# Strip copies on SyncE's queue: from the end of one turn to behind the next turn's map loads

## The chip, the cores and the metric

The kernel runs on one core of one Trainium2 chip. The metric is the device time of one execution in microseconds (us), lower is better. Everything is float32. The engines are PE (matrix), DVE (vector), ACT (scalar), POOL (GpSimd) and SP (SyncE, which only issues DMAs here). PEld is PE's weight load. DMAs are issued from SP, ACT and POOL. The profile shows three queues for them: q1 carries what SP issues, q10 what ACT issues, q0 what POOL issues. All three share the core's 16 DMA engines.

## The reference

The input x is 16 samples of 128 channels of 160 x 160 pixels. Per sample:

```python
x_proj = einsum('bchw,oc->bohw', x, proj_w)          # 128 -> 64 channels
att1 = _route(x_proj, ..., [3x3, 5x5], dilation 1)   # depthwise, one of two kernels
att2 = _route(att1, ..., [7x7, 9x9, 11x11], dilation 3)
out = concatenate([att1, att2], axis=1)
att = concatenate([out.mean(1), out.max(1)])         # two maps
att = sigmoid(conv7x7(att, sp_w) + sp_b)
gate = att[:, 0:1] + att[:, 1:2]
return out * gate + x
```

`_route` takes the mean of its input over all pixels, multiplies it with a small matrix, and uses the depthwise kernel of the largest logit. So the first convolution of a sample can't begin before the whole sample has been read and summed.

## The kernel before

The samples are pipelined in 18 turns, s = 0 to 17. In turn s, PE does in this order: the projection of sample s (`project`, L958, and the transposes `turn_x`, L967, in 30 pieces, five for each of six bands of rows), the routing of sample s (`route`, L1002 and L1009), the first convolution of sample s (`conv1`, L1022 and L1023, 32 pairs of channels) and then the second convolution of sample s-1 (`conv2`, L1086). Between the pairs of the first convolution stand the finishing steps of older samples: `finish2` (L1054 on PE, L1395 on DVE) gates the second half of the output of sample m = s-2 and adds x, `finish1` (L1065, L1420) does this for the first half of sample n = s-3. Turns 3 to 15 do all of this for new samples, thirteen turns. Turn 2 has no `finish1`. Turn 16 has no new sample but still a second convolution, turn 17 has neither.

The gate of sample m is made at the beginning of turn s. PE turns the two maps of sample m (`turn_map2`, L979), DVE writes them to Mt (`spread2`, L1337), SP stores Mt to map2_d in DRAM with twelve small DMAs (`store_map2`, L439), before these it reads the maps of the first half (L430), and behind them it reads the maps back in another layout (`load_maps`, L445). DVE joins both (`combine`, L1343 to L1346). PE convolves (`spatial`, L1032), ACT takes the sigmoid (L855), DVE adds (`sum_gate`, L1350). SP stores the gate (L465) and loads it with six DMAs in a third layout (L473). DVE copies it (`spread_gate`, L1358), PE turns it (`turn_gate`, L1040) and DVE takes it (`take_gate`, L1368). PE executes `turn_gate` behind the fourth pair of the first convolution, so a late gate stops the first convolution there. On DVE, `combine` stands ahead of the last band's sum (`take_x`, L1206 to L1211), and this stands ahead of the routing.

The bands 3 to 5 of x are loaded by POOL (L643) at the beginning of the turn: bands 3 and 4 at once, band 5 after band 3 has been used. ACT loads the first convolution's weights for five pairs ahead as soon as the routing is done (`load_w1`, L827), and in the second convolution it loads the weights of each pair (`load_w2`, L861).

Between the two convolutions a sample goes through DRAM. SP stores the first convolution's result to nat_d (`store_att1`, L488). `make_strips` (L538) then copies nat_d to strip_d, DRAM to DRAM, as 18 DMAs of 6.4 MB together. `land` (L478) loads strip_d into L for the second convolution. `land(s-1, u)` needs L freed by `finish2` and so comes in pieces late in the next turn. Before, `make_strips(s)` is SP's last step in turn s: behind `early_pieces` (L495, L502, L508), which run with the end of the second convolution. The next turn's `store_map2` follows on the same queue.

`wait_alone(engine, semaphore, value)` lets an engine wait. SP executes its list in order, so what stands behind a wait is issued after it.

Of the kernel before, what the change touches and what calls it, by code (L numbers as in the profile page):

```python
# [80 lines left out]
def conv_block(nc, x, proj_w, w1, b1, w2, b2, att1_w, att1_b, att2_w, att2_b, sp_w, sp_b, out):  # L81
    B = x.shape[0]
    ctx = ExitStack()
    with ctx:
# [188 lines left out]
        def wait_alone(eng, s, value):  # L273

            if isinstance(value, int) and value <= 0:
                return
            eng.wait_ge(s, value)
            eng.sem_inc(waits_met)
# [87 lines left out]
        def row_groups(r):  # L366

            return ((0, 48), (48, 6 if r == 0 else 5))
# [4 lines left out]
        def _(sp):  # L373
# [47 lines left out]
            def store_map2(m):  # L421

                for mm in range(2):
                    wait_alone(sp, map2_evac, 6 * m + 3 * mm + 3)
                    if mm == 0:
                        if isinstance(m, int) and m == 0:
                            sp.wait_ge(s_zeroed, 16 * NZ)
                        wait_alone(sp, map1_stored, 64 * (m + 1))
                        for k in range(2):
                            sp.dma_start(m1[64 * k:64 * k + 48, :, :],  # L430
                                         bass.AP(map1_d.tensor, m * (2 * 168 * W) + k * 168 * W, [[W, 48], [SPB * W, 4], [1, W]])
                                         ).then_inc(min_loaded, 16)
                    for cg in range(2):
                        for k in range(3):
                            n = 10 if (cg, k) == (1, 2) else 30
                            dst = bass.AP(map2_d.tensor, m * (2 * 168 * W) + (mm * 168 + 3) * W + 90 * cg + 30 * k,
                                          [[18 * W, BR], [W, 18], [1, n]])
                            src = Mt[k:NT:3, mm, 540 * cg:540 * cg + 540].rearrange("p (r j) -> p r j", j=30)[:, :, 0:n]
                            sp.dma_start(dst, src).then_inc(map2_stored, 16)  # L439

            def load_maps(m):
                wait_alone(sp, map2_stored, MP2 * (m + 1))
                wait_alone(sp, sp_mm, 2 * m)
                for k in range(2):
                    sp.dma_start(minc[64 * k:64 * k + 48, :, 3:3 + W],  # L445
                                 bass.AP(map2_d.tensor, m * (2 * 168 * W) + k * 168 * W, [[W, 48], [SPB * W, 4], [1, W]])
                                 ).then_inc(min_loaded, 16)

            def load_xf(m, u):
                for par in range(2 if u < 4 else 1):  # L450
                    n = min(ROWS2, H - 36 * u - 18 * par)
                    sp.dma_start(xf[u % 2][64 * par:64 * par + 64, 0:n * W],
                                 x[m, C2:C, 36 * u + 18 * par:36 * u + 18 * par + n, :].rearrange("c h w -> c (h w)")
                                 ).then_inc(xf_loaded[u % 2], 16)

            def store_xf(m, u):
                sp.wait_ge(f2_add, 45 * m + 9 * (u + 1))
                for par in range(2 if u < 4 else 1):
                    n = min(ROWS2, H - 36 * u - 18 * par)
                    sp.dma_start(out[m, C2:C, 36 * u + 18 * par:36 * u + 18 * par + n, :].rearrange("c h w -> c (h w)"),  # L460
                                 xf[u % 2][64 * par:64 * par + 64, 0:n * W]).then_inc(out2_stored[u % 2], 16)

            def load_gate(m):
                wait_alone(sp, gate_sum, m + 1)
                sp.dma_start(gate_d[m, 0:H, :].rearrange("(b i) w -> i b w", i=SPB),  # L465
                             sg[:, 0, :].rearrange("p (b w) -> p b w", w=W)).then_inc(gate_stored, 16)
                wait_alone(sp, gate_stored, 16 * (m + 1))
                for cg in range(2):
                    for k in range(3):
                        n = 10 if (cg, k) == (1, 2) else 30  # L470
                        src = bass.AP(gate_d.tensor, m * (168 * W) + 90 * cg + 30 * k, [[18 * W, BR], [W, 18], [1, n]])
                        dst = Gt[k:NT:3, 540 * cg:540 * cg + 540].rearrange("p (r j) -> p r j", j=30)[:, :, 0:n]
                        sp.dma_start(dst, src).then_inc(g2_loaded, 16)  # L473

            def land(s, bc):
                for p, po, r, lo, hi in ((0, 0, 0, 0, 192), (1, 0, 0, 192, 320), (1, 128, 1, 0, 64), (2, 0, 1, 64, 256)):
                    src = bass.AP(strip_d.tensor, (p * BK + bc) * 54 * 1920 + po, [[192, PB], [6 * 1920, BR], [1, hi - lo]])
                    sp.dma_start(Lc[64 * r:64 * r + PB].rearrange("p (n f) c -> p n (f c)", f=5)[:, BR * bc:BR * bc + BR, lo:hi],  # L478
                                 src).then_inc(landed, 16)
# [47 lines left out]
            def make_strips(s):  # L527
                wait_alone(sp, landed, LND * s)
                if isinstance(s, int) and s == 0:
                    sp.wait_ge(s_zeroed, 16 * NZ)  # L530
                for p in range(3):
                    for p0, n in row_groups(p):
                        d0 = p * BK * 54 * 1920 + p0 * 1920
                        f0 = s * (PIX * C2) + (p + 3 * p0) * W * C2
                        for do, fo, strips, run in ((54 * 1920, 15 * C2, 4, 1920), (15 * C2, 0, 1, 960), (5 * 54 * 1920, 135 * C2, 1, 1600)):
                            mid = [[54 * 1920, strips]] if strips > 1 else []
                            mid2 = [[1920, strips]] if strips > 1 else []
                            sp.dma_start(bass.AP(strip_d.tensor, d0 + do, [[1920, n]] + mid + [[1, run]]),  # L538
                                         bass.AP(nat_d.tensor, f0 + fo, [[3 * W * C2, n]] + mid2 + [[1, run]])).then_inc(strip_stored, 16)

            def load_g1(m):
                wait_alone(sp, pr_ready, 16 * m)
                sp.dma_start(G1[:, :, :, :].rearrange("p u r j -> p (u r) j"),
                             bass.AP(gate_d.tensor, m * (168 * W), [[10, PX1], [800, 32], [1, 10]])).then_inc(g1_loaded, 16)

            def turn(t):
                s, m = t.s, t.m
                if t.two:
                    store_map2(m)
                    load_maps(m)  # L550
                    if t.new:

                        wait_alone(sp, x_summed, NB1 * s + NB1 - 1)
                        wait_alone(sp, proj_mm, NF * (NB1 * s + NB1 - 1))
                    load_xf(m, 0)
                    load_gate(m)
                    wait_alone(sp, g2_mm, m + 1)
                    load_xf(m, 1)
                    if not t.new and not t.conv2:
                        load_g1(m)  # L560
                    if t.conv2:
                        wait_alone(sp, strip_stored, SST * s)
                    for u in range(NU2):
                        store_xf(m, u)
                        if t.conv2:
                            land(s - 1, u)
                        if u < 3:
                            wait_alone(sp, out2_stored[u % 2], xf_count(m, u))
                            load_xf(m, u + 2)
                    if t.conv2:  # L570
                        land(s - 1, 5)
                elif t.conv2:

                    sp.wait_ge(s_ones, 1)
                    wait_alone(sp, strip_stored, SST * s)
                    for bc in range(BK):
                        land(s - 1, bc)
                if t.new:
                    store_att1(s)
                if t.two and (t.new or t.conv2):  # L580
                    load_g1(m)
                if t.new:
                    wait_alone(sp, att1_stored, ST1 * (s + 1))
                    wait_alone(sp, red1_steps, s + 1)
                    if t.early:
                        begin_early(m)
                    if t.next:
                        load_x2(s + 1)
                    if t.early:
                        early_pieces(m)  # L590
                    make_strips(s)

            samples(sp, turn)
            for q in range(2):
# [937 lines left out]
```

## Time and profile before

| | us |
|---|---|
| median of three runs | 6009.83 |
| lowest and highest | 5991.84, 6009.97 |
| the profiled execution | 6016.42 |
| its span | 6014.7 |
| PE busy | 4768.7 (79%) |
| DVE busy | 3136.8 (52%) |
| ACT busy | 2827.8 (47%) |
| POOL busy | 1039.5 (17%) |

Times in the trace count from the start of the span. The beginning of a turn is best read from DVE's last `spread2` instruction (L1337): its end is called S here. At S the maps of sample m stand in Mt and can be stored. S is 3385.5 in turn 10, 600.1 in turn 2 and 5484.8 in turn 16. "S + 73.8" is a time 73.8 us after that.

### The profile page before, as it was taken

How to read it: one execution, taken by the hardware profiler on the slowest of the kernel's cores; microseconds unless marked ns; L12 is line 12 of the kernel's file. 1: busy time of each engine (PE TensorE's matmuls, PEld its weight loads, DVE VectorE, ACT ScalarE, POOL GpSimd, SP SyncE). 2: the span in 40 equal slices, each digit the busy share in tenths (PEclk: the TensorE clock that was granted, in tenths of full speed). 3: DMA queues.
4: the chain of work that ended last, by engine and by line, in shares of the span. 5: the costliest groups of instructions: out<-in, count | busy, mean ns of one | idle time of the engine just before them, and what ended most of it. 6: DMA issues, size and time to landing. Idle time of an engine off the chain costs nothing.

```text
span 6014.7 us, 156600 instructions
## 1 busy us (share of the span) xinstructions
PE 4768.7 (79%) x62816; PEld 3244.4 (54%) x62816; DVE 3136.8 (52%) x3931; ACT 2827.8 (47%) x5378; POOL 1039.5 (17%) x1574
## 2 busy tenths in 40 slices
PE   5678887888878888887888888788888878885453
PEld 2336474655647465564746547474654747464453
DVE  3315455554645546474554547455464755545345
ACT  3455554544545454454545454454545445451120
POOL 2001011111112111121211111121111212111232
PEclk8889999988989989898999989899998989897675
DMA  9655787979888797988879788897978888796957
GB/s 241 185 159 172 173 209 226 230 219 224 237 210 218 216 233 218 222 244 209 218 219 235 216 222 244 200 227 213 237 219 222 246 202 224 211 213 176 221 135 198
DMA packets 1033176, 1284.58 MB, mean 214 GB/s; under 512 B 670749, under 2 KB 865736, under 8 KB 1001885
## 3 DMA queue, kind: packets, MB, share of 16 engines
q1 hardware_dynamic: 899468, 723.43, 50.5%
q0 software_dynamic: 64304, 410.01, 21.8%
q10 hardware_dynamic: 69026, 146.11, 9.5%
q8 instruction: 235, 3.85, 0.3%
q14 instruction: 143, 1.17, 0.1%
HBM read 950.16 MB, written 456.70 MB: 234 GB/s over the span
## 4 chain that ended last, share of the span: by engine, by line
PE 50%; DMA 21%; SPq 9%; DVE 8%; issue 7%; ACT 3%; ACTq 1%; POOL 1%; another core or an unknown queue 0%; DVEq 0%; POOLq 0%
PE psC L1086 19%; PE psA L1022 10%; PE psA L1023 9%; DMA RX<-w_d 6%; SPq L439 6%; DMA RX<-in_x_dram 5%; PE psB L1054 3%; PE psA L958 3%; PE psB L1065 2%; PE psB L1032 2%; DMA out_dram<-RX 2%; DMA RX<-nat_d 2%; DVE L L1375 2%; PE psB L967 2%; DMA map_d<-RX 2%
## 5 line engine op out<-in xcount | busy, mean ns | idle before, releaser
L1086 PE MATMUL psC<-RX 61*60 61x96 f32 (+7 forms) x49152 | 1479.9, 268 | 276.1 <-POOL RX L680 129.4
L1086 PEld LDWEIGHTS psC<-RX 61*60 61x60 f32 x49152 | 1412.8, 134 | 341.9 <-issue 329.2
L875 ACT ACTIVATE L<-psC 124x120 f32 (+4 forms) x2048 | 396.8, 287 | 885.6 <-PE psC L1086 830.5
L1022 PE MATMUL psA<-X,RX 128*128 128x240 f32 x1280 | 638.0, 588 | 129.7 <-ACT RX L840 128.2
L680 POOL COPY RX<-RX 64x720 f32<-64x720 f32 x512 | 426.2, 839 | 1408.8 <-DMA RX<-w_d 1407.5
L845 ACT ACTIVATE X<-psA,bias 128x246 f32<-128x246 f32 x1024 | 626.6, 722 | 56.2 <-issue 25.6
L1054 PE MATMUL psB<-ident,L 124*128 124x124 f32 x2160 | 381.1, 318 | 334.9 <-DVE RX L1395 163.7
L1310 DVE TENSOR_REDUCE MM<-L 124x135 f32<-124x2160 f32 (+1 forms) x192 | 535.3, 2844 | 212.7 <-ACT L L875 212.7
L1395 DVE TENSOR_TENSOR RX<-psB,RX 128x360 f32<-128x360 f32 (+7 forms) x1200 | 359.2, 350 | 546.5 <-PE psB L1054 485.6
L1023 PE MATMUL psA<-X,RX 128*128 128x240 f32 x1280 | 632.5, 583 | 0.0
L865 ACT ACTIVATE RX<-L 128x1080 f32 (+1 forms) x256 | 542.4, 2127 | 147.8 <-DMA L<-strip_d 147.7
L958 PE MATMUL psA<-RX,projt 128*64 128x512 f32 x1600 | 460.4, 657 | 158.1 <-DMA RX<-in_x_dram 102.7
L834 ACT ACTIVATE RX<-RX 32x640 f32<-32x640 f32 x320 | 234.5, 737 | 744.6 <-PE psA L1023 665.3
L1054 PEld LDWEIGHTS psB<-ident,L 124*128 124x128 f32 x2160 | 295.7, 167 | 470.4 <-issue 460.3
L1286 DVE TENSOR_REDUCE MM<-X 128x246 f32<-128x15744 f32 x16 | 264.8, 16553 | 465.6 <-ACT X L845 465.6
L798 ACT ACTIVATE RX<-psA 128x512 f32<-128x512 f32 x480 | 287.9, 600 | 451.3 <-PE psA L958 407.5
L967 PEld LDWEIGHTS psB<-ident,RX 128*128 128x128 f32 x1920 | 209.2, 145 | 459.2 <-ACT RX L798 358.1
L1022 PEld LDWEIGHTS psA<-X,RX 128*128 128x128 f32 x1280 | 261.2, 223 | 314.6 <-issue 299.7
L1023 PEld LDWEIGHTS psA<-X,RX 128*128 128x128 f32 x1280 | 287.0, 224 | 226.7 <-issue 206.1
L1420 DVE TENSOR_TENSOR RX<-psB,RX 128x400 f32<-128x400 f32 x260 | 139.3, 571 | 506.0 <-PE psB L1065 505.2
L1022 PE MATMUL psA<-X,MM 128*128 128x240 f32 x768 | 381.5, 586 | 14.4 <-ACT MM L840 11.8
L1023 PE MATMUL psA<-X,MM 128*128 128x240 f32 x768 | 379.6, 583 | 0.0
(122 smaller groups left out, 5008.2 us busy)
## 6 DMA issues: line engine op xcount, KB each, us to landing
RX<-in_x_dram POOLq DMA_DIRECT2D x48, 2560.0 KB, 15.2
RX<-w_d ACTq DMA_DIRECT2D x512, 180.0 KB, 4.4
RX<-in_x_dram SPq DMA_DIRECT2D x128, 720.0 KB, 9.1
out_dram<-RX SPq DMA_DIRECT2D x128, 720.0 KB, 8.4
nat_d<-X SPq DMA_DIRECT2D x320, 280.0 KB
L<-strip_d SPq DMA_DIRECT2D x192, 405.0 KB, 10.5
strip_d<-nat_d SPq DMA_DIRECT2D x48, 1440.0 KB
RX<-nat_d POOLq DMA_DIRECT2D x130, 400.0 KB, 5.1
```

Of the source, the lines that this page charges most:

```text
L439: sp.dma_start(dst, src).then_inc(map2_stored, 16)
L680: nc.gpsimd.tensor_copy(w2t[j][64:128, :, :], w2t[j][0:64, :, :]).then_inc(w2_doubled, 1)
L845: ins = nc.scalar.activation(X[:, :, :, c:c + 1].rearrange("p b t c -> p (b t c)"), psA[pair % 2][:, ch * N1:(ch + 1) * N1], ACT.Identity, ...
L865: nc.scalar.activation(binf[q].rearrange("p (c f n) -> p c f n", c=G, f=5), Lc[:, :, bass.ds(g * G, G)].rearrange("p (n f) c -> p c f n", ...
L875: ins = nc.scalar.activation(dst[:, 0:NU2 - par, 15 * r:15 * r + nq, par, :], src[:, par:BR:2, :, :], ACT.Identity)
L958: ins = nc.tensor.matmul(o, projt[:, :], xsb[b][:, :, w0:w0 + FW], start=True, stop=True)
L1022: nc.tensor.matmul(o[:, :, 0:T1], w[:, ch, 96:224], rhs, start=True, stop=False, skip_group_check=True)
L1023: ins = nc.tensor.matmul(o[:, :, 1:1 + T1], w[:, ch, 224:352], rhs, start=False, stop=True, skip_group_check=True)
L1054: ins = nc.tensor.transpose(psB[t % 2][:, 124 * f:124 * f + 124], L[0:124, slot * C2:slot * C2 + 128], ident[0:124, 0:124])
L1086: ins = nc.tensor.matmul(o[:, :, 0:kk, a:b], w2t[2 * q + p][rows, ch, z:z + PB], src[rows, 2 * p + ch, 0:nf, 3 * cg + dc:3 * cg + dc + kk, ...
L1310: nc.vector.tensor_reduce(dst[0:124, mm, :].rearrange("p (f b k) -> p f b k", f=9, k=3)[:, :, par:BR:2, :], src[:, :, 0:NU2 - par, :, par, ...
L1395: return nc.vector.tensor_tensor(d, view(psB[t % 2][rows, :], 64 * g0 + c0, sdims), d, ALU.add)
```

## The change

`make_strips` is taken from the end of turn s and put into turn s+1, behind `load_maps(m)` where the turn has maps. In turn 1, which has none, it is put ahead of the wait on the strips, which is the place it had in effect. All its 18 DMAs and its wait on `landed` are the same. Nothing else is changed, and no other engine's instructions move.

```diff
@@ turn(t) of SP
                 if t.two:
                     store_map2(m)
                     load_maps(m)
+                    if t.conv2:
+                        make_strips(s - 1)
                     if t.new:
 
                         wait_alone(sp, x_summed, NB1 * s + NB1 - 1)
...
                 elif t.conv2:
 
                     sp.wait_ge(s_ones, 1)
+                    make_strips(s - 1)
                     wait_alone(sp, strip_stored, SST * s)
...
                     if t.early:
                         early_pieces(m)
-                    make_strips(s)
```

On SP, where one full turn ends and the next begins, before the change (the last store of `early_pieces`, then the strips; the maps follow behind all 18):

```order
L508 DMA out_dram<-X 64x800 [waits f1_add]
L508 DMA out_dram<-X 64x800
L538 DMA strip_d<-nat_d 48x4x1920 [waits landed]
L538 DMA strip_d<-nat_d 48x960
L538 DMA strip_d<-nat_d 48x1600
```

and with the change:

```order
L508 DMA out_dram<-X 64x800
L430 DMA RX<-map_d 48x4x160 [waits map2_evac,map1_stored]
L430 DMA RX<-map_d 48x4x160
L439 DMA map_d<-RX 162x1x30 x5
L439 DMA map_d<-RX 162x1x10
L439 DMA map_d<-RX 162x1x30 [waits map2_evac]
```

The maps now follow the early stores directly. On SP a little later in the same turn, around the loads of the maps and the gate, before the change:

```order
L439 DMA map_d<-RX 162x1x10
L445 DMA minc<-map_d 48x4x160 [waits map2_stored,sp_mm]
L445 DMA minc<-map_d 48x4x160
L452 DMA RX<-in_x_dram 64x2880 [waits x_summed,proj_mm]
L452 DMA RX<-in_x_dram 64x2880
L465 DMA gate_d<-RX 40x4x160 [waits gate_sum]
L473 DMA RX<-gate_d 9x18x30 [waits gate_stored]
```

and with the change, where the last of the 18 strip copies stands ahead of the loads of x for `finish2` (L452) and of the gate:

```order
L538 DMA strip_d<-nat_d 5x4x1920
L538 DMA strip_d<-nat_d 5x960
L538 DMA strip_d<-nat_d 5x1600
L452 DMA RX<-in_x_dram 64x2880 [waits x_summed,proj_mm]
L452 DMA RX<-in_x_dram 64x2880
L465 DMA gate_d<-RX 40x4x160 [waits gate_sum]
L473 DMA RX<-gate_d 9x18x30 [waits gate_stored]
```

The 18 copies have moved from between the early stores and the maps to between the maps and the gate.

## Rows read from the trace of the kernel before

**Rows 1.** The page: part 4 (shares of the last chain), part 6 (DMA issues).

```profile
PE 50%; DMA 21%; SPq 9%; DVE 8%; issue 7%; ACT 3%; ACTq 1%; POOL 1%; another core or an unknown queue 0%; DVEq 0%; POOLq 0%
...
RX<-in_x_dram SPq DMA_DIRECT2D x128, 720.0 KB, 9.1
```

**Rows 2.** Timeline of SP, turn 10: start, us, instruction, count, idle before.

```profile
3368.41 12.47 SPq L538 DMA_DIRECT2D strip_d<-nat_d  x18
...
3384.95 26.89 SPq L439 DMA_DIRECT2D map_d<-RX  x12
3417.23 0.80 SPq L445 DMA_DIRECT2D minc<-map_d  x2
...
3439.24 0.29 SPq L465 DMA_DIRECT2D gate_d<-RX  x1
3441.66 5.01 SPq L473 DMA_DIRECT2D RX<-gate_d  x6
```

**Rows 3.** Timeline of DVE, turn 10: maps spread (its end is S), gate taken.

```profile
3382.18 3.33 DVE L1337 TENSOR_TENSOR RX<-psC,mask 27x180 f32<-27x180 f32 x12 [2.16 <-PE psC L979]
...
3459.30 1.01 DVE L1368 COPY G2s<-psB 60x135 f32<-60x135 f32 x4 [7.63 <-PE psB L1040]
```

**Rows 4.** Timeline of PE, turn 10: band 3 begins, routing, first pair.

```profile
3397.48 1.98 PE L958 MATMUL psA<-RX,projt 128*64 128x512 f32 x4 [5.51 <-DMA RX<-in_x_dram]
...
3427.04 0.27 PE L1002 MATMUL psA<-stats,projt 128*64 128x25 f32 x2 [2.09 <-DVE stats L1216]
...
3443.42 1.14 PE L1022 MATMUL psA<-X,RX 128*128 128x240 f32 x2 [6.23 <-ACT RX L840]
```

**Rows 5.** Timeline of DVE, the gate taken in turns 3 and 15.

```profile
995.77 1.00 DVE L1368 COPY G2s<-psB 60x135 f32<-60x135 f32 x4 [7.37 <-PE psB L1040]
...
5217.27 1.00 DVE L1368 COPY G2s<-psB 60x135 f32<-60x135 f32 x4 [7.79 <-PE psB L1040]
```

**Rows 6.** Timeline of SP, turn 2.

```profile
624.23 0.80 SPq L445 DMA_DIRECT2D minc<-map_d  x2
...
649.67 4.81 SPq L473 DMA_DIRECT2D RX<-gate_d  x6
```

**Rows 7.** Timeline of PE, turn 2: band 3 begins, routing, first pair.

```profile
606.82 1.08 PE L958 MATMUL psA<-RX,projt 128*64 128x512 f32 x4 [0.28 <-DMA RX<-in_x_dram]
...
635.10 0.27 PE L1002 MATMUL psA<-stats,projt 128*64 128x25 f32 x2 [2.20 <-DVE stats L1216]
...
651.45 1.14 PE L1022 MATMUL psA<-X,RX 128*128 128x240 f32 x2 [6.20 <-ACT RX L840]
```

**Rows 8.** Timeline of DVE, turn 2: maps spread, gate copied, gate taken.

```profile
596.75 3.33 DVE L1337 TENSOR_TENSOR RX<-psC,mask 27x180 f32<-27x180 f32 x12 [2.26 <-PE psC L979]
...
655.99 1.49 DVE L1358 COPY RX<-RX 27x120 f32<-27x120 f32 x9 [8.79 <-DMA RX<-gate_d]
...
666.24 1.01 DVE L1368 COPY G2s<-psB 60x135 f32<-60x135 f32 x4 [8.76 <-PE psB L1040]
```

**Rows 9.** Landing of the load of the weights L861, 500 to 530 us and 530 to 545.

```profile
DMA to landing us min/median/max: 3.7/4.0/4.3
...
DMA to landing us min/median/max: 7.2/7.8/8.4
```

**Rows 10.** Timeline of SP, turn 16: strips, loads of the gate.

```profile
5469.97 12.65 SPq L538 DMA_DIRECT2D strip_d<-nat_d  x18
5483.42 0.97 SPq L430 DMA_DIRECT2D RX<-map_d  x2
...
5527.96 2.47 SPq L473 DMA_DIRECT2D RX<-gate_d  x3
```

**Rows 11.** DMA issues by line, 5483 to 5485 us: KB each, median us to landing.

```profile
RX<-map_d SPq DMA_DIRECT2D x2, 120.0 KB, 17.0
```

**Rows 12.** Timeline of DVE, turn 16: maps spread, gate copied, gate taken.

```profile
5481.55 3.29 DVE L1337 TENSOR_TENSOR RX<-psC,mask 27x180 f32<-27x180 f32 x12
...
5537.99 1.43 DVE L1358 COPY RX<-RX 27x120 f32<-27x120 f32 x9 [4.36 <-DMA RX<-gate_d]
5540.73 1.00 DVE L1368 COPY G2s<-psB 60x135 f32<-60x135 f32 x4 [1.30 <-PE psB L1040]
```

## The prediction

> **What bounds the kernel now.** I read the page's chain of work first [rows 1]. PE has half of the span in it, but DMA has 21% and SP's own issuing 9%. So the kernel is a chain through several engines, and a change on SP's queue can move it. Next I read the beginning of one full turn, turn 10, on SP, DVE and PE. The reader is to see four things there, all counted from S.
>
> First, SP issued the 18 strip copies in 12.5 us, ahead of S [rows 2]. Behind them the twelve small map stores took 26.9 us to issue, and the maps could be read back only at S + 31.7 [rows 2, 3]. Second, band 3 of x came late: PE stood 5.5 us for it [rows 4]. Third, the routing matmul ran at S + 41.5 after 2.1 us of waiting for DVE, whose last sum stands behind the joining of the maps, and the first convolution began at S + 57.9 [rows 4]. Fourth, the gate was taken at S + 73.8, and DVE had waited for PE there, not for the gate's loads [rows 3]. Everything that finishes old samples follows on this point. The gates taken in turns 3 and 15 are 4221.5 us apart [rows 5], 351.8 for each of the 12 turns between, so turn 10 can stand for the thirteen full turns. I price the change by what it does to this one point, "gate taken".
>
> **Natural experiments in the trace.** Turn 2 shows the beginning of a turn without strips in flight, since its strips were copied well inside the second convolution of turn 1. There the maps were read back at S + 24.1 instead of 31.7 [rows 6, 8], PE stood 0.3 us for band 3 instead of 5.5, routing ran at S + 35.0 instead of 41.5, the first pair at S + 51.4 instead of 57.9 [rows 7, 4], and the gate was taken at S + 66.2 [rows 8]. Turn 2 has no `finish1` pieces. Between first pair and gate turn 10 needed 15.9 us and turn 2 14.8.
>
> **The change, part by part.**
>
> *Removed ahead of the maps.* The map stores and the loads of bands 3 and 4 no longer share the DMA engines with the strips. I take turn 2's value for this: routing at S + 35.0, 6.5 us earlier per full turn. It is not more, since even then DVE's sum comes last, by 2.2 us [rows 7]. PE's own projection is next.
>
> *Added behind the maps.* The 18 copies now are issued from about S + 25.2 (24.1 for turn 2's maps and 1.1 for issuing them). They cost the same 12.5 us of SP. SP has nothing else to issue then but the loads of x for `finish2`, which wait for DVE's sum at S + 35 anyway. But two things that were free of the strips are not any more.
>
> The first is the load of the first convolution's weights, right after the routing, about S + 46. The nearest rows are the loads of the second convolution's weights on the same queue. They landed in 4.0 us ahead of the strips of turn 1 and in 7.8 with them in flight [rows 9]. So +3.8, between nothing (the strips may thin out by then) and 4.7 (8.4 against 3.7). First pair at 51.4 + 3.8 = S + 55.2, gate taken 15.9 later at **S + 71.1**, between 67.3 and 72.0. This is the bound by PE.
>
> The second is the gate itself. Its store stands on SP's queue behind the strips and behind two loads of 720 KB. What a DMA behind the strips pays is seen in turn 16: two map loads of 120 KB issued at 5483.4 landed 17.0 us later [rows 10, 11], 30.4 us after the first strip copy. From S + 25.2 this makes S + 55.6. The two loads of 720 KB land after 9.1 us when alone [rows 1]. A bare store and its semaphore take 2.4 us (3439.24 to 3441.66 in rows 2), which is in the 30.4 already, so I add 6.7, with 0 and 9.1 as ends, because those DMA engines that finish their strips early can begin. Gate stored at S + 62.3. From there to DVE's copy of the loaded gate turn 2 took 6.3 us (649.67 to 655.99) and turn 16 10.0 (5527.96 to 5537.99) [rows 6, 8, 10, 12]. I take 7, nearer to turn 2, as there is little other traffic by then. From copy to taking the gate turn 16 needed 2.7, with PE free [rows 12]. Sum: 62.3 + 7 + 2.7 = **S + 72.0**, between 64.6 (55.6 + 0 + 6.3 + 2.7) and 77.4 (55.6 + 9.1 + 10.0 + 2.7).
>
> The later of the two decides: S + 72.0 against 73.8 now. That is 1.8 us earlier per full turn, 13 x 1.8 = **23 us**. Of the 6.5 us that the routing gains most is given back at the gate.
>
> On arbitration the rows show only that the load's landing doubles. The Trainium skill, page "DMA: Bandwidth & Descriptors", section "Queues, rings and completion order", says that each DMA engine goes round-robin between the queues, packet by packet, and takes the descriptors of one queue in order. By that rule a small load on ACT's queue would pay less than I put down, and the gate behind the strips on SP's own queue would pay in full. The sum would stay at the gate's S + 72.0. The bound by PE would lie further below it, and I would give rival B's first condition more and its second less.
>
> *Turn 2* gets the strips of sample 1 into its beginning, which it was free of. By the same sums PE's bound is 66.2 + 3.8 = S + 70.0. The gate comes a little ahead of 72.0, as POOL has no loads of its own then. Cost 4, between 0 and 9.
>
> *Turn 16* has no new sample. Its gate was taken at S + 55.9 and was already last, as DVE and then PE waited for its loads [rows 12]. Now its maps are free of the strips, but the gate store is behind them. I estimate the reading back of the maps at S + 14: twelve stores at the 0.7 us that one strip copy takes SP (12.65 / 18, rows 10) are 8.4, and the rest is landing, under POOL's loads. The strips start at S + 15, 30.4 + 6.7 + 7 + 2.7 later is S + 61.8. Cost 6, between -6 (strips no longer in the way at all) and 10.
>
> *Turn 1* loses the strips of sample 1 from its second convolution, where weight loads landed in 7.8 instead of 4.0 [rows 9]. Five loads fell into that stretch and four buffers hide part of it. Gain 3, between 0 and 5.
>
> *The end of every other turn* loses nothing: the early stores and loads are issued ahead of the strips before, and PE then projects from bands that are already loaded. `land` needs the strips only behind the first store of `finish2`, more than 80 us after S. I price both at nothing. If the strips were not there by then, SP would stand at that wait with the x stores of `finish2` behind it.
>
> Sum: -23 + 4 + 6 - 3 = -16 us. The profiled execution took 6016.4, so 6000 for it. It was 6.6 us above the median, so against the median of 6009.8 I predict **5994 us**.
>
> **The rivals.**
>
> *B, the gain is kept.* The strips thin out before S + 46, the weights load as fast as now, and the gate is in time. The gate is then taken at 51.4 + 15.9 = S + 67.3, 6.5 us earlier, 13 x 6.5 = 85 us, and with turn 1 and turn 16 at even the time is about 5925. For it: between the loads of x and the routing little else asks for the DMA engines, so the strips begin at once. Against it: in turn 16 the strips kept a later DMA of their queue back for 30 us [rows 10, 11]. It needs both conditions, the gate stored by S + 58.
>
> *C, slower: the gate's DMAs become the bound.* The place is the store of the gate on SP's queue behind 6.4 MB of strips and 1.4 MB of x. It decides from the point at which the gate is stored later than S + 64, since 7 + 2.7 later is 73.8. The middle of its upper half is S + 75.6, 1.8 us later than now, 13 x 1.8 = 23, plus 6 for turn 2, 9 for turn 16, less 3: +35, about 6045. At its end of 77.4 it is 13 x 3.6 = 47 more, about 6070. For it: turn 16, where DVE waited for the gate even without strips behind the maps. Against it: in turn 10 DVE still waited 7.6 us for PE after copying the gate [rows 3], so it has slack.
>
> *D, the maps are not sooner.* Small stores alone, among the loads of x, could take as long as now. Then the routing gains nothing, the strips begin only at S + 33, and everything is as in C. I count it there. Turn 2's S + 24.1 speaks against it.
>
> **How the numbers follow.** Forecast 0.42, from 5970 to 6018 (1.8 us per full turn more or less). B with the cases between it and the forecast 0.33. C with D 0.25. Less than 0.3% (18 us) can hardly be told from no change here: the borders are 5992 and 6028. Faster: 0.33 from B and 0.11 of the forecast, 0.44. Slower: C and D with all but a little, 0.23, and 0.02 of the forecast's edge, 0.25. Same: the rest, 0.31. The range takes in B's price and C's: 5920 to 6048.
>
> **What would show it.** In the changed kernel's profile, counted from S: the map loads (L445) at 24 and no stall in the map stores beyond turn 2's; PE's wait for band 3 under 1 us; routing at 35; PE's wait for ACT ahead of the first pair some 4 us longer than the 6.2 of now [rows 4, 7]; the gate's loads (L473) beginning about S + 62, with DVE's copy (L1358) and PE's `turn_gate` (L1040) now waiting for them; gate taken about S + 72. I am wrong on the side of B if L1368 stands under S + 69 in the full turns, and on the side of C if over S + 74. If the first convolution and the finishing steps between gate and second convolution (some 150 us) change their length, a step is missing from this sum.

## The result: slower by 1.0%

| | before | changed |
|---|---|---|
| median, us | 6000.84 | 6060.12 |
| lowest and highest | 5987.93 to 6009.97 | 6053.26 to 6064.7 |
| runs | 4 | 4 |
| the profiled execution | 6016.42 | 6058.79 |
| its span | 6014.7 | 6057.0 |

The ratio is 1.0099, with a 95% interval of 1.0073 to 1.0125. The change costs some 59 us. The prediction was 5994, a small gain, with a range of 5920 to 6048, and 6060 lies above all of it. Rival C, the gate's DMAs behind the strips, had the right sign and place, but it was not the whole cause.

The page of the changed kernel, part 4: the chain that ended last, by engine and by line. (Lines from 551 on stand two further down than in the kernel before at most places: L958 is now L960, L1368 is L1370.)

```profile
PE 52%; DMA 24%; DVE 8%; issue 6%; SPq 4%; ACT 3%; POOL 1%; ACTq 1%; another core or an unknown queue 0%; POOLq 0%; DVEq 0%
PE psC L1088 20%; PE psA L1024 9%; PE psA L1025 9%; DMA RX<-in_x_dram 7%; DMA RX<-w_d 5%; PE psA L960 4%; PE psB L1056 3%; PE psB L969 2%; DMA out_dram<-RX 2%; PE psB L1067 2%; PE psB L1034 2%; DMA gate_d<-RX 2%; DMA RX<-nat_d 2%; DVE L L1377 2%; DVE MM L1312 2%
```

Against [rows 1] SP's issuing fell from 9% to 4%, as the map stores no longer stall behind the strips. DMA rose from 21% to 24%, and the gate's store (`gate_d<-RX`) now is in the list with 2%. The gain and the loss can both be seen in these two lines.

SP's waits, the row of the gate's store, of the kernel before and of the changed one: in total, times, longest.

```profile
SPq L278 <- DMA gate_d<-RX: 33.5, 16, 3.0
```

```profile
SPq L278 <- DMA gate_d<-RX: 289.6, 16, 23.5
```

SP waited 2.1 us for each store of the gate before, and 18.1 after.

Now turn 10 of the changed kernel, whose S is 3406.79 (3403.47 + 3.32), to be laid beside [rows 2 to 4]. The timeline of SP:

```profile
3405.36 0.80 SPq L430 DMA_DIRECT2D RX<-map_d  x2
3406.20 15.56 SPq L439 DMA_DIRECT2D map_d<-RX  x12
3423.15 0.81 SPq L445 DMA_DIRECT2D minc<-map_d  x2
3424.07 12.82 SPq L538 DMA_DIRECT2D strip_d<-nat_d  x18
3437.08 1.16 SPq L452 DMA_DIRECT2D RX<-in_x_dram  x2
3450.65 0.29 SPq L465 DMA_DIRECT2D gate_d<-RX  x1
3471.32 5.23 SPq L473 DMA_DIRECT2D RX<-gate_d  x6
```

The map stores take 15.6 us and not 26.9, and the maps are read back at S + 16.4 and not 31.7. The strips begin at S + 17.3. The gate's store is issued at S + 43.9, nearly 10 us earlier than before, but its loads follow only at S + 64.5, 8 us later than before.

The timelines of DVE and of PE, the same turn:

```profile
3403.47 3.32 DVE L1339 TENSOR_TENSOR RX<-psC,mask 27x180 f32<-27x180 f32 x12 [4.52 <-PE psC L981]
...
3480.09 1.47 DVE L1360 COPY RX<-RX 27x120 f32<-27x120 f32 x9 [9.57 <-DMA RX<-gate_d]
3482.44 1.00 DVE L1370 COPY G2s<-psB 60x135 f32<-60x135 f32 x4 [0.88 <-PE psB L1042]
```

```profile
3430.70 1.08 PE L960 MATMUL psA<-RX,projt 128*64 128x512 f32 x4 [1.49 <-DMA RX<-in_x_dram]
3439.45 0.30 PE L1004 MATMUL psA<-stats,projt 128*64 128x25 f32 x2
...
3463.61 1.14 PE L1024 MATMUL psA<-X,RX 128*128 128x240 f32 x2 [15.00 <-ACT RX L842]
...
3481.70 0.70 PE L1042 MATMUL psB<-ident,RX 27*124 27x27 f32 x9 [0.40 <-DVE RX L1360]
```

Band 3's wait of 5.5 us is gone altogether (for band 5 PE now stands 1.5 us), and the routing runs at S + 32.7 in place of 41.5 [rows 3, 4]. Then PE stands 15.0 us for ACT, where it stood 6.2 [rows 4]. ACT in its turn waits for the weights of the first convolution. The first pair is at S + 56.8, only 1.1 us earlier than before. And now DVE waits 9.6 us for the gate's loads, so the gate is taken at S + 75.7, against 73.8 [rows 3].

What these two DMAs meet is seen in a table of the stretch, four windows of 10 us: the last columns are PE's granted clock, the share of the DMA engines that is busy, and what they move.

```profile
3424.00:3434.00 10.00, 8.51 (x46) 3.38 (x46) 3.08 (x9) 6.33 (x12) 0.00 (x0) 1.00 1.00 376
3434.00:3444.00 10.00, 9.19 (x43) 4.62 (x44) 6.40 (x21) 4.71 (x9) 3.42 (x6) 1.00 1.02 340
3444.00:3454.00 10.00, 4.61 (x22) 2.46 (x20) 4.54 (x17) 2.08 (x4) 1.29 (x3) 0.94 1.01 282
3454.00:3464.00 10.00, 0.39 (x1) 0.42 (x2) 1.49 (x1) 2.62 (x4) 0.38 (x1) 0.50 1.05 246
```

For 40 us all the DMA engines are full, from the first strip to the first pair. The time of the first weight load (3449.6) and of the gate's store (3450.65) lies in the middle. PE's busy time falls to 0.39 us in the last window, in which its clock also is at its lower level (0.50 of full speed, 1.2 GHz) after standing still.

The landing of the five weight loads of turn 10 (line L829, min, median, max in us):

```profile
DMA to landing us min/median/max: 10.8/13.1/15.1
```

They landed in 2.0 us before (median of the five of turn 10).

The means over the thirteen full turns, from the same timelines, in us. "Its result" is DVE's last step of the routing, the cast that gives the index of the kernel to use (L1278, now L1280), and ACT asks for the weights some 2 us later. The rows add up to the whole turn, from one S to the next:

| stretch | before | changed |
|---|---|---|
| S to routing (L1002) | 41.7 | 34.3 |
| routing to its result | 8.4 | 8.0 |
| result to first pair (L1022) | 7.4 | 15.6 |
| first pair to gate taken (L1368) | 15.9 | 18.0 |
| gate taken to second convolution | 148.5 | 148.4 |
| second convolution to the next S | 128.9 | 129.1 |
| whole turn | 350.8 | 353.5 |

So 7.4 and 0.4 us are won, 8.2 are lost to the weights and 2.1 to the gate, and the rest of the turn doesn't change. 13 x 2.7 is 35 of the 42.3 us between the two profiled spans. Turn 2 is 0.7 shorter, turn 16 is 2.5 longer, the last turn 0.5. The remaining 4.8 lie ahead of turn 2's S (604.9 against 600.1). I don't put them down to the change: in the six kernels below whose turn 1 is the same as the changed kernel's, that S stands at 597.2 to 602.8. Turn 1 scatters by some us from one execution to the next.

### The profile page after: what moved, and what is told of

Read it like the earlier page. It is cut to its first block, busy times and chain, and to the rows that moved or that the text cites. A ratio compares the mean times of both kernels' runs of the same rounds, so it can differ in the third digit from the quotient of the medians.

```text
span 6057.0 us, 156601 instructions
## 1 busy us (share of the span) xinstructions
PE 4732.6 (78%) x62816; PEld 3234.8 (53%) x62816; DVE 3138.5 (52%) x3931; ACT 2820.5 (47%) x5378; POOL 1040.2 (17%) x1574
## 4 chain that ended last, share of the span: by engine, by line
PE 52%; DMA 24%; DVE 8%; issue 6%; SPq 4%; ACT 3%; POOL 1%; ACTq 1%; another core or an unknown queue 0%; POOLq 0%; DVEq 0%
PE psC L1088 20%; PE psA L1024 9%; PE psA L1025 9%; DMA RX<-in_x_dram 7%; DMA RX<-w_d 5%; PE psA L960 4%; PE psB L1056 3%; PE psB L969 2%; DMA out_dram<-RX 2%; PE psB L1067 2%; PE psB L1034 2%; DMA gate_d<-RX 2%; DMA RX<-nat_d 2%; DVE L L1377 2%; DVE MM L1312 2%
## 5 line engine op out<-in xcount | busy, mean ns | idle before, releaser
L1088 PE MATMUL psC<-RX 61*60 61x120 f32 (+7 forms) x49152 | 1475.5, 267 | 282.0 <-POOL RX L682 114.9
L960 PE MATMUL psA<-RX,projt 128*64 128x512 f32 x1600 | 451.3, 645 | 98.5 <-DMA RX<-in_x_dram 41.9
```

Of the source, the lines that this page charges most:

```text
L960: ins = nc.tensor.matmul(o, projt[:, :], xsb[b][:, :, w0:w0 + FW], start=True, stop=True)
L1088: ins = nc.tensor.matmul(o[:, :, 0:kk, a:b], w2t[2 * q + p][rows, ch, z:z + PB], src[rows, 2 * p + ch, 0:nf, 3 * cg + dc:3 * cg + dc + kk, ...
```

## The experiments

Every edit is against the changed kernel, except where it says otherwise. Means are over the thirteen full turns of the profiled execution. "Before" was run beside each, and a ratio is to it. A kernel without a ratio was executed once, and executions of "before" lie up to 40 us apart, so of such a kernel the means by turn say more than the time. All the changes between these kernels are in the order of SP's list, in what is copied, or in who issues the gate.

### Strips behind the gate

```diff
                     load_maps(m)
-                    if t.conv2:
-                        make_strips(s - 1)
...
                     load_xf(m, 0)
                     load_gate(m)
+                    if t.conv2:
+                        make_strips(s - 1)
```

> The 18 strip copies are issued behind the loads of the gate (L473) and no longer ahead of them; the rest is the changed kernel. Theory 1: the changed kernel loses at two DMAs that meet the strips in flight, the first convolution's weights (13 us to landing in place of 2) and the gate's store (20 us in place of 2.4). Then here weights land in about 2 us again, the first pair stands at about S + 50, the gate is stored in under 4 us and taken at about S + 65, some 11 us earlier per full turn than in the changed kernel and 8 earlier than before, so about 5900 us, if the finishing steps behind the gate are as long as now (some 150 us). Rival 2: the DMA engines are the bound of the whole turn, and 6.4 MB cost the same wherever they stand. Then what is gained up to the gate is lost between gate and second convolution, and the time stays near 6000.

5964.8 us, ratio to before 0.9927 (0.9899 to 0.9955). The landing of the weights in turn 10, and PE's first pair:

```profile
DMA to landing us min/median/max: 2.0/2.0/2.8
```

```profile
3390.63 0.30 PE L1004 MATMUL psA<-stats,projt 128*64 128x25 f32 x2
...
3406.02 1.14 PE L1024 MATMUL psA<-X,RX 128*128 128x240 f32 x2 [6.22 <-ACT RX L842]
```

Weights in 2.0 us, PE's wait back at 6.2, gate taken at a mean of S + 65.6, 7.8 us ahead of before, as theory 1 said. But the time is 65 us above its 5900. The stretch from gate to second convolution grew from 148.5 to 151.7, and the next one by 0.8. So both theories hold in part: the loss ahead of the gate is the strips' meeting with two urgent DMAs, and about half of the gain is given back where the strips stand now, beside the finishing steps.

### No strips

```diff
-                for p in range(3):
+                for p in range(3 if s == 0 else 0):
...
-                        wait_alone(sp, strip_stored, SST * s)
+                        wait_alone(sp, strip_stored, SST + 96 * 0 * (s - 1))
```

> The changed kernel, but only sample 0's strips are copied; for samples 1 to 15 the copies are left out (the second convolution reads sample 0's strips, the output differs from the reference). It measures what the copies cost in all. Theory 1: first pair at S + 49 to 51, gate taken at S + 64 to 66, as in turn 2 of the kernel before, in every full turn: about 5890 us or less. Rival 2 expects the finishing steps between gate and second convolution to become shorter too, by 10 us or more per turn, and a time under 5800. If the gate is still taken after S + 74, neither theory holds.

5909.4 us. Result to first pair 7.3, gate taken at S + 65.6, gate to second convolution 149.2, not shorter. Rival 2 falls: the DMA engines do not bound the turn as a whole. The strips cost only where they stand in somebody's way. It also gives the floor: the strips' price in the kernel before is some 95 us (6004.2 for "before" beside it, less 5909.4, with the noise of one execution).

### A third of the strips

```diff
-                for p in range(3):
+                for p in range(3 if s == 0 else 1):
...
-                        wait_alone(sp, strip_stored, SST * s)
+                        wait_alone(sp, strip_stored, SST + 96 * 1 * (s - 1))
```

> The changed kernel with a third of the copies: sample 0's strips in full, then only the first of the three tables for each sample (6 DMAs, 2.1 MB; the output differs from the reference). A dose test. Theory 1: the third starts at S + 19 and is through by about S + 32, ahead of the routing's end. So weights land in 2 to 5 us, the gate's store in 3 to 6, first pair near S + 51, gate near S + 67: nearly all of the loss gone with two thirds of the copies. If the cost were in proportion to the bytes (rival 2), the gate would be taken near S + 69 to 72, a third of the way from no strips to all.

5916.5 us. Result to first pair 8.9 in the mean, gate at S + 66.8. The loss is not in proportion: one third of the bytes brings 1.5 of 8.2 us. It is a matter of time. In the turns whose third began at S + 18 to 20 (eight of thirteen), the result and the first pair are 7.3 to 8.2 apart. In the five whose third began at S + 25 to 26 they are 9.5 to 11.7 apart.

Yet even in those five the copies themselves are over when the weights are asked for. In turn 4 that is at 1305.2 (S + 44.4). The DMA queues in the 4 us behind it (packets, MB, share of the 16 engines):

```profile
q0 software_dynamic: 189, 0.79, 92.2%
q10 hardware_dynamic: 33, 0.07, 6.9%
q1 hardware_dynamic: 13, 0.01, 1.0%
```

q1, with strips and loads of x, is next to empty. q0 fills the engines. This is mostly POOL's loads for the first `finish1` pieces (L693, L700), issued at S + 35 to 38, and the five weight loads landed in 6.9 to 7.4 us. The gate's store, issued at 1306.02, was followed by its first load only at 1314.84, 8.8 us later. In the other four late turns q1 has 0 to 4% in these 4 us and q0 64 to 95%. Without any strips, q0 is empty there in every full turn. So the copies need not be in flight themselves at S + 43. It is enough that they have pushed other loads to that time.

### The loads of x behind the gate

```diff
-                    load_xf(m, 0)
                     load_gate(m)
+                    load_xf(m, 0)
```

> The changed kernel, but the two loads of x for the finishing steps (1.4 MB, L452) are issued behind the gate's store and loads, not ahead. The strips stay ahead of both. Theory 1 with the sum's term for these loads (6.7 us): the gate is stored at about S + 58 in place of S + 64, DVE no longer waits for it, and the gate is taken when PE allows, 16 us after the first pair at S + 57, so at S + 73, 3 us earlier per full turn: about 6020 us. If the loads of x don't hold the gate back, nothing moves: 6060. If they come too late for the first finishing step, it moves the other way.

5988.1 us, ratio to before 0.9971 (0.9957 to 0.9985), and 72 us below the changed kernel, where 40 were expected. The gate gained 1.4 of its 2.1 us: 16.6 us from first pair, in place of 18.0, where some 16 were expected. What I had not expected is that the weights gained more. Turn 10's five:

```profile
DMA to landing us min/median/max: 6.4/8.4/10.2
```

Result to first pair fell from 15.6 to 11.5. So of the 8.2 us that the weights lost, 4.0 were due to the 1.4 MB of x that stood between the strips and the gate, and only the other 4.2 to the strips, with POOL's loads beside them.

### The same exchange in the kernel before

```diff
-                    load_xf(m, 0)
                     load_gate(m)
+                    load_xf(m, 0)
```

> The kernel before, strips at their old place, but with the loads of x for the finishing steps (L452) issued behind the gate's store and loads. It is the control for the same exchange made in the changed kernel, which brought 5.0 us per full turn there. Theory 1: the exchange helps only where strips fill the queue ahead of it. At the old place the loads of x are through before the routing is done, the weights land in 2 us and the gate's store in 2.4 anyway, so nothing is gained: 5995 to 6015 us. It could lose 1 or 2 us per turn if the loads of x come too late for the first finishing step. If it gains more than 1 us per turn, the loads of x are a cost of their own.

6016.4 us, ratio 1.0011 (0.9994 to 1.0028), every stretch within 0.3 us of before. The loads of x are no cost of their own. They cost only when the strips have pushed them on to the routing's end.

### The strips behind the loads of x

```diff
                     load_maps(m)
-                    if t.conv2:
-                        make_strips(s - 1)
...
                     load_xf(m, 0)
+                    if t.conv2:
+                        make_strips(s - 1)
                     load_gate(m)
```

> The changed kernel, but the strips are issued behind the loads of x for the finishing steps (L452), still ahead of the gate's store. They begin at S + 35 and not at S + 18 to 25. Theory 1, with the sizes of the traces since: the weights' loads, asked for at S + 43, meet strips in full flight, so some 8 us late again, first pair about S + 57. The gate's store is behind strips that began 10 to 17 us later, so it is stored about S + 70 to 75 in place of 64, and the gate is taken at S + 82 to 87: 6 to 11 us later per full turn than in the changed kernel, 6140 to 6200 us. It tells the two victims apart: the weights' delay should not grow, the gate's should. If the gate is taken as early as in the changed kernel, the order on SP's own queue is not what holds it.

6023.2 us, and the expectation was wrong by more than 100 us, to the wrong side. I had read the wait ahead of `load_xf` as one for the last band. It is for band 4. The loads of x went out at once and the strips began at S + 23 to 28, in the mean only 6 us later than in the changed kernel. So the test wasn't the one I wanted. What it shows all the same: the weights now pay 11.0 (not 15.6) and the gate 19.9 (not 18.0). With x out of the way of both, the strips and POOL's loads take 3.6 us from the weights, which agrees with the 4.2 above, and the gate is the later one.

### The gate on POOL's queue

```diff
# SP
-                    load_gate(m)
# POOL, between begin1 and the pieces; load_gate as before, issued by pool
+                if t.two:
+                    load_gate(t.m)
```

> The changed kernel, strips in the new place, but the gate's store and its six loads are issued by POOL and not by SP, so they stand on another queue than the strips. It takes one of the two victims out of the strips' queue and leaves the other. Theory 1: the weights stay late (16 us from the routing's end to the first pair, as in the changed kernel). The gate's store pays as the weights' loads do, some 10 to 15 us in place of 20, so its copy on DVE is no longer last, and the gate is taken 15.8 us after the first pair, at about S + 74 in place of 76: 6020 to 6040 us. The 2.1 us lost between first pair and gate are then the gate's own part, and the 8 us ahead of the first pair are the weights'. If the gate is still stored 20 us after it is asked for, the DMA engines as a whole hold it and not the order on SP's queue.

6060.4 us, no gain, where 20 to 40 us were expected. First pair to gate is 15.7 us, so the gate's own part is gone, as expected. Turn 10's gate store, by its line: time to landing.

```profile
DMA to landing us min/median/max: 9.7/9.7/9.7
```

On SP's queue 20.7 us passed in turn 10 from the store to the first load of the gate. Here it is 10.4, though the DMA engines are as full until then. Over the full turns it was 16.6 to 20.7 there, and the store landed in 8.9 to 13.5 here. So some half of the gate's delay came from standing behind the strips on SP's queue. (The run changes the queue and the engine that issues together.) Result to first pair is 14.2, so 6.8 of the 8.2 us stay with the weights. But a third victim came up: S to routing is 37.7 in place of 34.3. In turns 8, 9, 11, 13 and 15 the routing is at S + 41 to 44, and there PE waits for band 5 of x. Turn 8:

```profile
2722.97 1.97 PE L974 MATMUL psA<-RX,projt 128*64 128x512 f32 x4 [6.16 <-DMA RX<-in_x_dram]
```

Its band 5 landed 12.3 us after it was asked for, where turn 8 of the changed kernel has 7.5. The timelines of SP and of POOL, turn 8:

```profile
2709.95 13.22 SPq L538 DMA_DIRECT2D strip_d<-nat_d  x18
```

```profile
2710.63 0.53 POOL L644 DMA_DIRECT2D RX<-in_x_dram  x1 [0.79 <-DVE part L1227]
```

In exactly these five turns SP issued its first strip 0.3 to 0.9 us ahead of POOL's load of band 5. Routing then followed 20.9 to 23.2 us after that load was issued. In the changed kernel the load was ahead of the first strip in every turn, by 0.8 us or more (turn 8: 2712.44 against 2714.71), and routing followed 16.0 to 19.2 us after it. So a microsecond between two queues, which nothing in the program fixes, goes with some 5 us of a turn (22.3 against 17.0 us in the mean from band 5's load to the routing). In the run with a third of the strips the load was 0.4 us ahead in turn 13, and landed in 7.9 us.

The order is not all of it. In the same five turns POOL asked for band 5 at S + 20.3 to 20.9, in the mean 3.3 us later than in the changed kernel, having issued band 3 at S - 0.8, where every other full turn of these two kernels has S - 2.3 or earlier. Why POOL was later there, and whether the gate's DMAs in its list have to do with it, was not followed. So the routing's loss of 3.4 us in the mean can't be put down to the order alone, nor kept apart from POOL's queue.

### Strips in two parts

```diff
                     load_gate(m)
+                    if t.conv2:
+                        make_strips(s - 1, (2,))
...
                         early_pieces(m)
+                    make_strips(s, (0, 1))
```

Here `make_strips` takes the tables that it copies. The second run has `(0,)` at the end of the turn and `(1, 2)` behind the gate. In both, the copies behind `load_maps` are gone, and in turn 1 the later part alone stands ahead of the wait on the strips.

> Strips in two parts: two of the three tables (12 DMAs, 4.2 MB) at the old place at the end of the turn, the third (2.1 MB) behind the loads of the gate. Theory 1: the stretch from S - 17 to S - 2.5, in which the loads of x have not begun, is free for strips and holds about two thirds of them (they moved some 0.3 MB a us in turn 16); the last third then collides little with the finishing steps. So routing at S + 35 to 36, first pair at S + 51, gate at S + 66 to 68, and the stretch from gate to second convolution 149 to 150 us and not the 151.7 of all strips behind the gate. That gives 5 to 7 us per full turn below the kernel before: 5915 to 5945 us, under the 5965 of all strips behind the gate. If two thirds still stand in the way of the maps and of band 3, routing is at S + 38 or later and the time at 5960 or above.

> As the run with two tables at the old place, but with one there (6 DMAs, 2.1 MB) and two behind the loads of the gate (4.2 MB). Theory 1: the head of the turn is fully free, routing at S + 34.5, gate at S + 66. The two tables behind the gate cost two thirds of the 3.2 us that all three cost there, so about 345.5 us per full turn and 5940 us in all. If the cost behind the gate isn't in the bytes, it stays 151.7 us from gate to second convolution and the time near 5960.

Two early: 5945.0 us, ratio 0.9879 (0.9848 to 0.9909). One early: 5908.2 us, ratio **0.982** (0.9791 to 0.9849). The second beats both kernels, by 105 us against before. Its median is that of the kernel without strips. But the execution of it that was profiled is the slowest of its four (5930.0, from 5899.5), 21 us above the one of the kernel without strips, and its full turns are 345.2 us against 344.1. So a cost of up to 1.1 us per turn isn't excluded. Its turn 10 on SP:

```profile
3318.09 4.16 SPq L538 DMA_DIRECT2D strip_d<-nat_d  x6
...
3359.41 0.80 SPq L445 DMA_DIRECT2D minc<-map_d  x2
3360.40 1.19 SPq L452 DMA_DIRECT2D RX<-in_x_dram  x2
3381.35 0.28 SPq L465 DMA_DIRECT2D gate_d<-RX  x1
3383.62 4.81 SPq L473 DMA_DIRECT2D RX<-gate_d  x6
3388.55 9.30 SPq L538 DMA_DIRECT2D strip_d<-nat_d  x12
```

and its windows from the first strips on (the last two columns: busy share of the DMA engines, GB/s):

```profile
3317.00:3322.00 5.00, 5.00 (x28) 1.99 (x28) 5.00 (x5) 3.70 (x7) 0.00 (x0) 1.00 0.96 283
3322.00:3327.00 5.00, 5.00 (x27) 1.85 (x24) 4.92 (x6) 3.73 (x7) 0.00 (x0) 1.00 0.88 284
3327.00:3332.00 5.00, 5.00 (x32) 2.51 (x29) 2.73 (x8) 3.73 (x7) 1.64 (x3) 1.00 0.13 42
```

One table is through by about 3327, in front of the loads of x that POOL issues some 6 us later. Two tables are not quite: routing is at S + 36.9 in place of 34.6. Behind the gate, two tables leave 149.2 us to the second convolution, the same as without any, where three made 151.7. My expectation there (two thirds of the 3.2 us) was too dear. The cost behind the gate is not in proportion to the bytes either. Which transfer of the finishing steps the third table meets was not tried.

## Why the prediction was wrong

*The head of the turn.* Right, with turn 2 as the model: routing at S + 35.0 predicted, 34.3 measured. The maps came back even earlier than in turn 2 in most turns, so the strips began at S + 17 to 25 and not at 25.2. That was no gain, since routing then hangs on band 5. One reading was wrong here: the loads of x do not wait for DVE's sum at S + 35 but for band 4, and in turn 2 they had gone out at S + 25.2. It did no harm to the sum, as they stand behind the strips in it either way.

*The weights.* This is the step that failed first. I took +3.8 us, with 4.7 as the end, and 8.2 were measured. The rows behind it were right, but they were of one load at a time beside the strips alone. In the changed kernel the DMA engines hold the strips, POOL's loads and 1.4 MB of x at that moment, and ACT asks for six DMAs at once. The exchange of the loads of x shows the parts: 4.2 us for the strips with POOL's loads, and 4.0 for the loads of x, which my sum let wait only in front of the gate and not in front of the weights. That the 4.2 is near my 3.8 is partly luck, since my rows had none of POOL's loads in them.

*The gate.* From the first strip to the gate's first load I had 37.1 us, and turn 10 shows 47.2. The model, turn 16, had neither band 5 nor the weights beside the strips. The strips' earlier start made up for most of that: S + 64.5 measured, 62.3 predicted.

*"The later of the two decides."* I had 71.1 for PE's bound and 72.0 for the gate's. With the weights' 8.2 PE's bound was 73.8 (34.3 + 8.0 + 15.6 + 15.9), above that of my gate and half a us later than the gate was taken before in the mean (73.3). The gate then added its 2.1. So the likeliest case had already lost all its gain at the weights. In place of 13 x 1.8 = 23 us won, the full turns lost 13 x 2.7 = 35. These 58 us are the miss of the profiled execution (6000 predicted, 6058.8 measured), all but a us. Rival C named only the gate. The run with the gate on POOL's queue shows that without its delay the first pair is still 7 us late.

*Turn 2* paid 3.9 us up to the gate, predicted 4, but the turn as a whole lost nothing. *Turn 16* paid 5.7 up to the gate (S + 61.6, predicted 61.8), of which 2.5 were left at the turn's end. *Turn 1*: 3 us of gain predicted. S of turn 2 stands at 597.2, 598.9, 599.7, 599.8, 602.7 and 602.8 in the six kernels with the same turn 1, at 604.9 in the changed kernel, and at 600.1 before. So whether it gained at all stays open. *The end of the turn and `land`*: rightly priced at nothing, 148.4 and 129.1 us against 148.5 and 128.9.

*The rule that the prediction weighed.* In turn 10 the first load of the gate followed its store by 20.7 us on SP's queue and by 10.4 on POOL's, with the strips in flight in both. The Trainium skill, page "DMA: Bandwidth & Descriptors", section "Queues, rings and completion order", says that each DMA engine takes the descriptors of one queue in order, and this agrees. ACT's small loads, on a queue of their own, landed in 13.1 us in place of 2.0. From the same section's taking of turns between queues I had read that they would pay less than I put down. They paid more, 8.2 us against 3.8: taking turns with two other queues that are full (q1 and POOL's q0) doesn't make a small DMA fast here.

## What to carry to other kernels

A bulk copy with slack belongs where no short DMA with a waiter is issued until it, and what it has pushed back, has drained. In this kernel moving it cost what was asked for while the DMA engines were full, some 40 us from its first DMA in turn 10, on any queue and not only on its own. List these DMAs, with everything else that the bulk pushes along, before pricing the move. And a bulk copy can be cut: a third in one gap and two thirds in another cost next to nothing here (at most some 20 us between the two profiled executions), while the whole cost some 55 us behind the gate (5964.8 against 5909.4, the one execution without strips), some 95 at its old place and some 150 at its new one.

## What was not expected of the hardware

With 6.4 MB of DRAM to DRAM copies, 1.4 MB of x and POOL's loads in flight, 88 KB loads from another queue landed in 10.8 to 15.1 us in place of 2 (turn 10). The DMA engines' share stayed at 1.0 while what they moved fell from 376 to 246 GB/s within 40 us, so a full share says little about how soon they will be free.

Nor had I expected that the order of two issues on different queues, a microsecond or two apart, would matter: band 5 of x landed in 6.9 to 8.8 us when asked for 0.8 us or more ahead of the strips (the full turns of the changed kernel), and in 10.5 to 12.3 us when asked for 0.3 to 0.9 us behind the first of them (five turns of the kernel with the gate on POOL's queue).
